# Gated cross-attention and a routed feed-forward layer: a second buffer of unloaded values, positions behind the maxima, tile rows loaded ahead of weights, tiles from the last values' round on

## The chip, the cores and the metric

The kernel runs on one core of a Trainium2 chip. The time is device microseconds from start to end of one execution; the number of the kernel before is the median of three. The engines are TensorE (PE in the profile, its weight loads PEld), VectorE (DVE), ScalarE (ACT), GpSimd (POOL) and the sync engine (SP), which here issues the plain transfers.

## What is computed

Inputs: x of 32 batches x 128 rows x 128 channels, a context of 32 x 120 x 128, one mask of 128 x 120, 16 heads of 8 channels, 8 experts of width 512. Cut to what matters:

```python
x = x + tanh(g_x) * attention(layernorm(x), ctx, ctx, mask)     # 16 heads, softmax over 120 keys
# feed-forward, top 2 of 8 experts, on all 4096 rows
x_flat = layernorm(x).reshape(T, d)
scores = x_flat @ gate_w + gate_b
topk_vals, topk_idx = top_k(scores, 2)
combine_w = zeros.at[tok, topk_idx].add(softmax(topk_vals))
h = relu(x_flat @ w1[e] + b1[e]);  y = h @ w2[e] + b2[e]        # for each expert e
x = x + tanh(g_f) * sum_e combine_w[:, e] * y[e]
```

The kernel computes only the two chosen experts of each row: the rows are scattered to lists in DRAM, one list for each expert (`zs`), read back in tiles of 256 rows, taken through one expert's weights, scattered to `res`, and added at the end.

## The kernel before, in words

**Attention.** 32 batches in 8 groups of 4. The program is written by hand as 38 rounds k = 0 to 37 on every engine (`round_`); G = k // 4 is the group and p = k % 4 the place in it. Round k < 32 takes the row maxima (VectorE, L1068), the exponentials (ScalarE, L819) and the transposes (TensorE, L632, into the banks T and U, copied out to `PT` by L1074 and L826) of batch k. It also takes the products with the values and the row sums of batch k-1 (L654, L664, bank O) and unloads them (`unload`: reciprocal L1080, product into `OT` L1084). At p = 1 TensorE multiplies the group's `OT` by the output weights (`proj_entry`, L673), and VectorE adds the residual (L1089).

**Routing.** For each group VectorE finds the top 2 (`route` parts 0 and 1), makes one-hots and running counts (part 2), adds the ranks that TensorE computed (`RANK`, part 3), makes the row numbers `posu` (part 4, L1142 to L1147) and the weights of the two experts (part 5, L1151 to L1154). GpSimd scatters the normalised rows with `posu` (L959), eight indirect transfers for a group.

**Tiles.** 39 tiles of 256 rows in two batches of tiles: 16 of the groups 0 to 5, and 23 of the rest. A batch's tables (`table` parts 0, 1 and 2, after the last group's ranks) say for each tile its expert and its first row. SP reads them and loads the weights of a tile (`load_w`, 578 KB, 4 buffers) and its rows (`load_z`, 132 KB, 6 buffers); both transfers stand in SP's one queue. TensorE takes a tile in two halves: transposes of the rows (L746), the first product with two banks of hidden values (L718), ScalarE's relu (L856), the second product (L740); VectorE copies the transposed rows (L1221, L1225) and writes the result (L1231), and GpSimd scatters it (L970). One half of a tile is a pair of steps; `PAIRS = 4` of them are planned into each round after the attention's end, up to round 37, and what is left follows. The first rows of a batch of tiles are transposed by opening steps (`PRE`) at the end of the round before the first planned pair.

**Banks.** Steps that are planned before round 33 (`LATE`) use bank O for the rows and results and bank U for the hidden values alone. From round 33 on, O and S0, and U and T, are used in turns.

**The end.** When all tiles are scattered, the results are read back in 16 parts and combined with the weights, and x is stored.

## Time and profile before

| | |
|---|---|
| median of 3 runs | 508.17 us (506.07 to 510.29) |
| the profiled execution's own time | 506.01 us |
| its span, first to last instruction | 504.2 us |
| TensorE busy | 418.4 us (83%) |
| VectorE, ScalarE, GpSimd busy | 268.6, 284.4, 271.8 us |
| mean granted TensorE clock | 0.931 of full speed |

The profile lists for each engine what it ran and when, and for an idle stretch what ended it ("issue" and "remote" are ends for which it shows no releasing instruction). Matmuls are pipelined, so durations of neighbours overlap by some tenths of a microsecond, and the distance between starts is the better measure of pace. Work of the attention rounds ends at about 300 us, tiles run from there to 478 us, and the combination of the results takes the rest.

### The profile page before, as it was taken

The page shows a single profiled execution, that of the slowest core. Times are in us where ns is not written, and L with a number is a line of the kernel's source. Part 1 is how long each engine was busy: PE and PEld are TensorE (multiplying, and loading weights), DVE is VectorE, ACT ScalarE, POOL GpSimd, SP SyncE. Part 2 cuts the span into 40 slices and gives each one's busy share as a digit, 9 for nine tenths or more (in the row PEclk, how much of TensorE's full clock was granted, in tenths as well). Part 3 has the DMA queues.
Part 4 walks back from the last instruction along what each step waited for, and adds up shares of the span by engine and source line. Part 5 has one row for each costly group of instructions (what it writes and reads, how often), then busy time and mean ns, then how long its engine had stood idle before and what let it go on. Part 6 is the DMA issues. An engine that isn't in the chain of part 4 may idle for free.

```text
span 504.2 us, 12347 instructions
## 1 busy us (share of the span) xinstructions
PE 418.4 (83%) x4299; PEld 333.3 (66%) x4299; DVE 268.6 (53%) x1010; ACT 284.4 (56%) x848; POOL 271.8 (54%) x297
## 2 busy tenths in 40 slices
PE   0779889999899999998988777988589999999900
PEld 0455667667667667576756466977479899999800
DVE  1345667777677676776667553433422333233247
ACT  1277868778787778786856711423133444444334
POOL 8536319059498496793942801864755355554500
PEclk9979999999999999999989956998879999999965
DMA  3999999500000000000010052555538677778278
GB/s 74 240 359 410 412 392 216 104 12 14 23 12 23 25 12 23 13 13 29 8 33 14 33 179 81 175 167 168 173 117 251 197 218 233 239 217 247 90 231 280
DMA packets 48155, 72.55 MB, mean 144 GB/s; under 512 B 8054, under 2 KB 32638, under 8 KB 48094
## 3 DMA queue, kind: packets, MB, share of 16 engines
q1 hardware_dynamic: 43549, 62.32, 40.6%
q0 software_dynamic: 4544, 9.45, 5.3%
q8 instruction: 35, 0.57, 0.5%
q14 instruction: 27, 0.21, 0.1%
HBM read 41.83 MB, written 34.66 MB: 152 GB/s over the span
## 4 chain that ended last, share of the span: by engine, by line
PE 74%; issue 8%; DVE 5%; DMA 4%; ACT 3%; SPq 3%; POOL 1%; another core or an unknown queue 1%; DVEq 0%; POOLq 0%; ACTq 0%
PE S L740 7%; PE T L718 7%; PE O L740 7%; PE U L718 7%; PE S L624 6%; PE O L664 6%; PE O L654 6%; PE T L632 6%; PE S L614 5%; PE U L632 5%; ACT P L819 2%; DMA yg<-res 2%; DVE PT L1074 2%; PE E L673 2%; PE E L688 2%
## 5 line engine op out<-in xcount | busy, mean ns | idle before, releaser
L819 ACT ACTIVATE P<-S,nmax 128x120 f32<-128x120 f32 x512 | 135.2, 420 | 6.9 <-DVE nmax L1068 5.4
L959 POOL DMA_INDIRECT zs<-z,posu x64 | 63.2, 988 | 99.6 <-DVE posu L1147 81.0
L970 POOL DMA_INDIRECT res<-yo,dpos x78 | 75.0, 961 | 64.7 <-DVE yo L1231 56.6
L1068 DVE TENSOR_REDUCE nmax<-S 128x4 f32<-128x480 f32 x128 | 75.1, 649 | 37.4 <-PE S L624 32.3
L826 ACT COPY PT<-U 120x512 f32<-120x512 f32 x64 | 39.6, 619 | 52.9 <-PE U L632 51.7
L856 ACT ACTIVATE H<-T,wbuf 128x256 f32<-128x256 f32 x78 | 32.7, 471 | 62.5 <-PE T L718 45.0
L614 PE MATMUL S<-mb_r,I_r 128*128 128x480 f32 x128 | 65.3, 514 | 2.1 <-ACT P L819 1.9
L856 ACT ACTIVATE H<-U,wbuf 128x256 f32<-128x256 f32 x78 | 32.7, 471 | 51.7 <-PE U L718 37.3
L938 POOL TENSOR_SCALAR Kb<-Kt,hm 128x480 f32<-128x480 f32 x32 | 47.0, 1482 | 18.2 <-ACT Kt L840 18.2
L928 POOL TENSOR_SCALAR z<-X,mv,rstd 128x128 f32<-128x128 f32 x64 | 50.2, 791 | 3.0 <-POOL rstd L923 2.7
L1080 DVE RECIPROCAL orec<-O 128x128 f32<-128x128 f32 x32 | 30.6, 957 | 39.2 <-PE O L664 39.2
L718 PE MATMUL T<-zT,wbuf 128*128 128x256 f32 x156 | 42.5, 397 | 6.8 <-issue 6.8
L740 PEld LDWEIGHTS S<-wbuf,H 128*128 128x128 f32 x312 | 42.1, 198 | 8.3 <-issue 6.2
L740 PE MATMUL S<-wbuf,H 128*128 128x128 f32 x312 | 43.4, 284 | 4.6 <-issue 2.9
L664 PE MATMUL O<-PT,oneV 120*32 120x128 f32 x1024 | 41.8, 279 | 5.6 <-issue 5.4
L632 PEld LDWEIGHTS U<-I,P 128*120 128x120 f32 x256 | 30.3, 142 | 24.2 <-issue 22.5
L632 PE MATMUL T<-I,P 128*120 128x128 f32 x256 | 40.9, 284 | 5.3 <-DVE PT L1074 4.1
L654 PE MATMUL O<-PT,Vm 120*32 120x128 f32 x1024 | 35.6, 279 | 11.0 <-issue 11.0
L740 PEld LDWEIGHTS O<-wbuf,H 128*128 128x128 f32 x312 | 41.0, 193 | 4.0 <-DVE yo L1231 2.0
L740 PE MATMUL O<-wbuf,H 128*128 128x128 f32 x312 | 41.6, 276 | 1.4 <-DVE yo L1231 1.4
L632 PE MATMUL U<-I,P 128*120 128x128 f32 x256 | 41.9, 288 | 0.0
L718 PE MATMUL U<-zT,wbuf 128*128 128x256 f32 x156 | 41.8, 392 | 0.0
(161 smaller groups left out, 654.0 us busy)
## 6 DMA issues: line engine op xcount, KB each, us to landing
wbuf<-wpk SPq DMA_DIRECT2D x39, 578.0 KB
zs<-zero SPq DMA_DIRECT2D x1, 17952.0 KB, 60.2
zin<-zs SPq DMA_DIRECT2D x39, 132.0 KB
yg<-res SPq DMA_DIRECT2D x16, 256.0 KB, 4.2
wpk<-in_w SPq DMA_DIRECT2D x1, 2048.0 KB, 57.7
wpk<-in_w SPq DMA_DIRECT2D x8, 256.0 KB, 9.3
out<-X SPq DMA_DIRECT2D x16, 128.0 KB, 3.4
ctx_sb<-in_ctx SPq DMA_DIRECT2D x1, 1440.0 KB, 16.8
```

The lines of the kernel that those rows point to most:

```text
L614: mm(Sb[n % NHG][:, 0:HG * LK].rearrange("p (j k) -> p j k", j=HG), I_r[:], mb_r[:].unsqueeze(1).broadcast_to((128, HG, LK)), start=True, ...
L632: last = nc.tensor.transpose(t_bank(n)[0:LK, j * LQ:(j + 1) * LQ], P[:, n % 4, j, :], I[:])
L654: mm(Ob[32 * j:32 * j + 32, 0:LQ], Vm[:, G % 2, i * HG + j, 32 * g:32 * g + 32], PT[:, (NHG * k + g) % NPT, j * LQ:(j + 1) * LQ], start=(g ...
L664: last = mm(Ob[32 * j:32 * j + 32, LQ:2 * LQ], oneV[:, g, :], PT[:, (NHG * k + g) % NPT, j * LQ:(j + 1) * LQ], start=(g == 0), stop=(g == ...
L718: last = mm(u_bank(a)[:, c * TS:(c + 1) * TS], wbuf[:, n % NW, h * 128:(h + 1) * 128], zT[:, n % 2, :], start=True, stop=True)
L740: last = mm(y[:, 2 * 128:3 * 128], H[:, n % 2, c, h * 128:(h + 1) * 128], wbuf[:, n % NW, FF + c * D:FF + (c + 1) * D], start=(c == 0), st ...
L819: ins = nc.scalar.activation(P[:, n % 4, j, :], a[:, j * LK:(j + 1) * LK], ACT.Exp, bias=nmax[:, n % 4, j:j + 1])
L856: nc.scalar.activation(H[:, n % 2, h, :], u_bank(a)[:, c * TS:(c + 1) * TS], ACT.Relu, bias=wbuf[:, n % NW, W_B1 + h:W_B1 + h + 1]).then_i ...
L928: ins = nc.gpsimd.tensor_scalar(dst[:, i, :], batch_x(G, i), mv[:, i, 0:1], r[:, 1, i:i + 1], ALU.subtract, ALU.mult)
L959: nc.gpsimd.indirect_dma_start(out=zs, out_offset=bass.IndirectOffsetOnAxis(ap=posu[:, F, k, i:i + 1], axis=0), in_=z2[:, F % 2, i, :], in ...
L970: nc.gpsimd.indirect_dma_start(out=res, out_offset=bass.IndirectOffsetOnAxis(ap=dpos[:, n % NDP, h:h + 1], axis=0), in_=yo[:, n % NYO, h, ...
L1068: v.tensor_reduce(nmax[:, n % 4, :], Sb[n % NHG][:, 0:HG * LK].rearrange("p (j k) -> p j k", j=HG), AX_X, ALU.max, negate=True).then_inc(m ...
```

## The change

- `OT` has two buffers, and the first unload of group G waits for the output product of group G-2, not G-1.
- On VectorE the row numbers (route part 4, at p = 1) and the expert weights (part 5, at p = 2) stand right behind the row maxima, ahead of the unload.
- The first batch's table part 2 is written in the same round as part 1 (round 30), not one round later.
- SP loads rows and weights of tiles in turns, rows first. The wait for the tables moves to the first rows' load, which also waits for the scatters of group 5.
- The first planned pair of steps is in round 32, the round of the last values, and the opening steps are at the end of round 31. So 24 of the 34 pairs of the first batch of tiles are planned into rounds, where there were 20; the number of pairs is the same.

```diff
--- before.py
+++ after.py
@@ -94,7 +94,7 @@
 
     subs, pre, k = {}, {}, 0
     for b in range(NB):
-        j, k = 0, max(k, GB * (LAST[b] + 1) + 5)
+        j, k = 0, max(k, GB * (LAST[b] + 1) + 4)
         if k < NR:
             pre[k - 1] = b
         while j < SUBS[b] and k < NR:
@@ -304,7 +304,7 @@
         P = sb("P", [128, 4, HG, LK])
         PT = sb("PT", [LK, NPT, HG * LQ])
         orec = sb("orec", [128, LQ])
-        OT = sb("OT", [128, TOK])
+        OT = sb("OT", [128, 2, TOK])
         xb = sb("xb", [128, GB, D])
 
         z2T = sb("z2T", [128, TOK])
@@ -511,8 +511,6 @@
             def load_w(n):
 
                 b, i = tile_of(n)
-                if i == 0:
-                    sp.wait_ge(table_step, NTAB * (b + 1))
                 wait(sp, yo_done, TH * (n - NW + 1))
                 e = sp.value_load(tab[0:1, b, 1, i:i + 1], min_val=0, max_val=NE - 1)
                 sp.dma_start(wbuf[:, n % NW, :], wpk[bass.ds(e, 1)].squeeze(0)).then_inc(w_in[n % NW], 16)
@@ -521,6 +519,7 @@
 
                 b, i = tile_of(n)
                 if i == 0:
+                    sp.wait_ge(table_step, NTAB * (b + 1))
                     for q in range(2):
                         sp.wait_ge(scat[q], 16 * 2 * GB * ((LAST[b] + 1 - q) // 2))
                 if n >= NZ:
@@ -550,12 +549,13 @@
                     known = N0[b + 1]
                     if b + 1 < NB and ROUND_OF.get((b, 2 * TH * (i + 1) - 1), NEVER) > GB * (LAST[b + 1] + 1) + 1:
                         known = N0[b + 2]
-                    while w_next < min(N0[b] + i + NW, known):
-                        load_w(w_next)
-                        w_next += 1
-                    while z_next < min(N0[b] + i + NZ, known):
-                        load_z(z_next)
-                        z_next += 1
+                    while z_next < min(N0[b] + i + NZ, known) or w_next < min(N0[b] + i + NW, known):
+                        if z_next < min(N0[b] + i + NZ, known):
+                            load_z(z_next)
+                            z_next += 1
+                        if w_next < min(N0[b] + i + NW, known):
+                            load_w(w_next)
+                            w_next += 1
             stored(sp, N0[NB])
             for u in range(NU):
                 load_results(u)
@@ -670,7 +670,7 @@
                 a = entry("PROJ", G)
                 pe.wait_ge(o_free, at(G, GB, GB) + 1)
                 for i in range(GB):
-                    last = mm(a[:, i * D:(i + 1) * D], OT[:, i * LQ:(i + 1) * LQ], wo_sb[:], start=True, stop=True)
+                    last = mm(a[:, i * D:(i + 1) * D], OT[:, G % 2, i * LQ:(i + 1) * LQ], wo_sb[:], start=True, stop=True)
                 last.then_inc(e_ready, 1)
 
             def z2_entry(F):
@@ -1079,9 +1079,9 @@
                 G, i = divmod(k, GB)
                 v.reciprocal(orec[:], Ob[:, LQ:2 * LQ]).then_inc(orec_done, 1)
                 dve.wait_ge(orec_done, k + 1)
-                if i == 0 and G >= 1:
-                    ready(dve, "PROJ", G - 1)
-                v.tensor_tensor(OT[:, i * LQ:(i + 1) * LQ], Ob[:, 0:LQ], orec[:], ALU.mult).then_inc(o_free, 1)
+                if i == 0 and G >= 2:
+                    ready(dve, "PROJ", G - 2)
+                v.tensor_tensor(OT[:, G % 2, i * LQ:(i + 1) * LQ], Ob[:, 0:LQ], orec[:], ALU.mult).then_inc(o_free, 1)
 
             def residual(G):
                 ready(dve, "PROJ", G)
@@ -1258,6 +1258,8 @@
                         row_max(NHG * k + g)
                 if p < 2 and first:
                     taken[first[0]](first[1])
+                if 0 < p < 3 and 0 <= G - 2 < NG:
+                    route(G - 2, 4 if p == 1 else 5)
                 if 0 <= k - 1 < B:
                     unload(k - 1)
                 step(ks[1:2])
@@ -1265,8 +1267,8 @@
                     copy_pt(NHG * k)
                 if middle:
                     taken[middle[0]](middle[1])
-                if p < 3 and 0 <= G - 2 < NG:
-                    route(G - 2, {0: 2, 1: 4, 2: 5}[p])
+                if p == 0 and 0 <= G - 2 < NG:
+                    route(G - 2, 2)
                 if p == 1 and G - 2 == NG - 1:
                     route(G - 2, 5)
                 step(ks[3:4])
@@ -1280,7 +1282,6 @@
                 step(ks[7:8])
                 if p == 2 and G - 1 in LAST and G < NG:
                     table(sb_of(G - 2), 1)
-                if p == 3 and G - 1 in LAST and G < NG:
                     table(sb_of(G - 2), 2)
                 if k in PRE:
                     for i, _ in OPENING:
```

TensorE's queue from the end of round 31 on. A line with - is the order before; `zin` rows are the tile rows' transposes, U and T with `I,P` the last transposes of the attention, O the values and sums.

```order
 L632 MATMUL T<-I,P 120x128 x4
-L632 MATMUL U<-I,P 120x128 x4
-L654 MATMUL O<-PT,Vm 32x128 x16
-L664 MATMUL O<-PT,oneV 32x128 x16
 L746 MATMUL O<-I,zin 128x128 x3
-L695 MATMUL E<-Mh,tri 128x32
-L696 MATMUL E<-CU,ones 128x32
-L718 MATMUL T<-zT,wbuf 128x256 x2
-L746 MATMUL S<-I,zin 128x128
-L673 MATMUL E<-wo_sb,OT 128x128 x4
-L718 MATMUL U<-zT,wbuf 128x256 x2
```

```order
+L632 MATMUL T<-I,P 120x128 x4
+L654 MATMUL O<-PT,Vm 32x128 x16
+L664 MATMUL O<-PT,oneV 32x128 x16
+L718 MATMUL U<-zT,wbuf 128x256 x2
+L746 MATMUL O<-I,zin 128x128
+L718 MATMUL U<-zT,wbuf 128x256 x2
+L746 MATMUL O<-I,zin 128x128
+L718 MATMUL U<-zT,wbuf 128x256 x2
+L740 MATMUL O<-wbuf,H 128x128 x4
```

The three opening transposes now stand ahead of the last attention transposes and values. Four halves of tiles, all with bank U, follow the sums directly, and the ranks and the output product of the last groups come after them.

SP's queue from the first load of a tile on, before:

```order
L517 TENSOR_LOAD tab [waits table_step,wpk_done]
L517 ISA x2
L518 ISA
L518 DMA wbuf<-wpk 128x1156
L517 TENSOR_LOAD tab
```

And with the change:

```order
L528 TENSOR_LOAD tab [waits scat0,scat1,table_step,wpk_done]
L528 ISA x2
L529 ISA
L529 DMA zin<-zs 128x2x132
L515 TENSOR_LOAD tab
L515 ISA x2
L516 ISA
L516 DMA wbuf<-wpk 128x1156
```

Before, four weight loads and then six row loads follow each other. Now the first load is one of rows, behind the table and behind the scatters (`scat0`, `scat1`), and weights and rows alternate.

VectorE's queue in round 29 (p = 1 of group 7), before:

```order
L1080 RECIPROCAL orec<-O 128x128
L1084 TENSOR_TENSOR OT<-O,orec 128x128
L1074 COPY PT<-T 120x512
L1089 TENSOR_TENSOR X<-E,xb 128x512
L1142 TENSOR_TENSOR pm<-hot,pe 128x64
L1143 TENSOR_REDUCE posf<-pm 128x8
L1145 COPY z<-tokf 128x4
L1146 COPY z<-idxf 128x4
L1147 CAST posu<-posf 128x8
```

And with the change:

```order
L1142 TENSOR_TENSOR pm<-hot,pe 128x64
L1143 TENSOR_REDUCE posf<-pm 128x8
L1145 COPY z<-tokf 128x4
L1146 COPY z<-idxf 128x4
L1147 CAST posu<-posf 128x8
L1080 RECIPROCAL orec<-O 128x128
L1084 TENSOR_TENSOR OT<-O,orec 128x128
L1074 COPY PT<-T 120x512
L1089 TENSOR_TENSOR X<-E,xb 128x512
```

The five instructions of `posu` moved from behind the residual to ahead of the reciprocal; the same happens in each p = 1 round from group 2 on.

## Rows read from the trace of the kernel before

**Rows 1.** The page, part 1: busy time, share of the span, instructions.
```profile
PE 418.4 (83%) x4299; PEld 333.3 (66%) x4299; DVE 268.6 (53%) x1010; ACT 284.4 (56%) x848; POOL 271.8 (54%) x297
```
**Rows 2.** The chain that ended last, 440 to 504 us: start, length, what.
```profile
461.69 0.86 PE T L718 x4
...
465.42 0.86 PE T L718 x4
...
479.42 2.23 DMA res<-yo,dpos
...
483.10 5.30 DMA yg<-res
```
**Rows 3.** TensorE in time, around the attention's end: start, length, instruction, [idle before].
```profile
294.31 1.08 PE L632 MATMUL U<-I,P 128*120 128x128 f32 x4
...
297.79 1.96 PE L664 MATMUL O<-PT,oneV 120*32 120x128 f32 x32
305.05 0.66 PE L746 MATMUL O<-I,zin 128*128 128x128 f32 x2 [5.30 <-DMA zin<-zs]
306.62 0.47 PE L746 MATMUL O<-I,zin 128*128 128x128 f32 x1 [0.91 <-DVE zT L1221]
...
307.18 2.05 PE L718 MATMUL T<-zT,wbuf 128*128 128x256 f32 x4
...
309.24 1.91 PE L673 MATMUL E<-wo_sb,OT 128*128 128x128 f32 x8
...
312.25 1.03 PE L718 MATMUL T<-zT,wbuf 128*128 128x256 f32 x4
```
**Rows 4.** SP's queue in time, the first loads of tiles.
```profile
294.64 3.73 SPq L518 DMA_DIRECT2D wbuf<-wpk  x4
299.20 6.59 SPq L530 DMA_DIRECT2D zin<-zs  x6
```
**Rows 5.** Busy time in stretches; last three columns: granted clock, DMA share, GB/s.
```profile
288.00:312.00 24.00, 16.59 (x118) 13.32 (x118) 9.13 (x47) 2.70 (x6) 1.69 (x2) 0.51 0.42 137
290.00:296.00 6.00, 5.39 (x26) 4.69 (x24) 4.42 (x28) 1.75 (x4) 0.00 (x0) 0.50 0.10 17
...
300.00:305.00 5.00, 0.00 (x0) 0.00 (x0) 2.31 (x9) 0.00 (x0) 0.00 (x0) 0.50 0.91 309
...
360.00:374.00 14.00, 7.81 (x32) 6.36 (x32) 1.65 (x10) 2.52 (x6) 8.30 (x10) 0.63 0.35 95
```
**Rows 6.** Who waited for whom over the span: us in total, times, longest.
```profile
DVE OT L1084 <- PE E L673: 6.0, 7, 0.9
...
PE T L632 <- DVE PT L1074: 4.1, 13, 0.4
```
**Rows 7.** VectorE in time, one p = 1 round of the attention.
```profile
199.61 0.96 DVE L1080 RECIPROCAL orec<-O 128x128 f32<-128x128 f32 x1 [1.42 <-PE O L664]
201.43 0.29 DVE L1084 TENSOR_TENSOR OT<-O,orec 128x128 f32<-128x128 f32 x1 [0.86 <-PE E L673]
```
**Rows 8.** TensorE in time, the same round.
```profile
202.46 0.62 PE L632 MATMUL T<-I,P 128*120 128x128 f32 x4 [0.27 <-DVE PT L1074]
```
**Rows 9.** VectorE in time, rounds 29, 31 and a round of tiles.
```profile
272.87 0.16 DVE L1147 CAST posu<-posf 128x8 uint32<-128x8 f32 x1
...
293.38 0.16 DVE L1195 TENSOR_TENSOR st<-end,nt 128x8 f32<-128x8 f32 x1
...
333.14 0.22 DVE L1214 SCALAR_TENSOR_TENSOR dsum<-zin,exf 128x2 f32<-128x2 f32 x1 [4.81 <-remote]
```
**Rows 10.** GpSimd in time: the last scatter of group 5.
```profile
287.46 0.96 POOL L959 DMA_INDIRECT zs<-z,posu  x1 [0.30 <-issue]
```
**Rows 11.** ScalarE in time: the second half's relu.
```profile
312.34 0.84 ACT L856 ACTIVATE H<-U,wbuf 128x256 f32<-128x256 f32 x2 [2.23 <-PE U L718]
```
**Rows 12.** VectorE in time, behind round 37.
```profile
364.95 0.16 DVE L1218 TENSOR_TENSOR dpos<-dsum,own 128x2 uint32<-128x2 f32 x1 [6.89 <-remote]
```
**Rows 13.** GpSimd in time: the last scatter of group 7.
```profile
361.75 0.96 POOL L959 DMA_INDIRECT zs<-z,posu  x1 [0.30 <-issue]
```

## The prediction, made before the changed kernel ran

> **What bounds the kernel now.** I began with the page. TensorE is busy 83% of the span [rows 1], so it is the engine to follow, and I read the chain that ended last. In its last third it is TensorE alone, and from the first half of one tile to the first half of the next it takes 465.42 - 461.69 = 3.73 us [rows 2]. At that pace 39 tiles are 145.5 us. The first product of a tile starts at 307.18 us [rows 3], and the read-back that follows the last tile's scatter starts at 483.10 us [rows 2]. The tiles' stretch is therefore some 30 us longer than its pace, and only such excess, or an idle place before 307 us, can be won. Nothing in the change touches the pace, and nothing touches the 21 us behind 483 us.
>
> Next I went through TensorE in time around the attention's end. The last transposes start at 294.31, the last sums end at 299.76, and then the engine stands still for 5.30 us until the first tile rows land, and for another 0.91 us on VectorE's copy of them [rows 3]. SP's queue says why: the tables are finished at 293.54 [rows 9], four weight loads of 578 KB are issued from 294.64, and the first rows only from 299.20 [rows 4]. While TensorE stands, the DMA engines are 91% busy at 309 GB/s [rows 5]: the rows wait behind 2.3 MB of weights. Last I read the granted clock: from 288 to 312 us it is 0.51, that is the lower of the two levels, 1.2 GHz, and TensorE is busy 16.59 us in it [rows 5]. About half of that, 8.3 us, is what the slow clock costs.
>
> **The change, part by part.**
>
> *Second buffer of `OT`.* In seven p = 1 rounds VectorE waits for the output product before it may write `OT`, 6.0 us in all [rows 6]. In the round shown the wait is 0.86 us [rows 7], and behind it stands the copy of `PT`, for which TensorE then waits 0.27 us [rows 8]. VectorE itself has slack elsewhere. So I count TensorE's wait: 7 x 0.27 = 1.9 us, which with the waits at p = 0 (these stay) makes up the 4.1 us of 13 waits [rows 6]. Bounds: 0, if TensorE waits a little later for ScalarE instead, and 6.0, if all of VectorE's wait reached the end. I take **-1.9**, since TensorE's own row is nearest.
>
> *Positions and expert weights behind the maxima.* Part 4 takes some 0.7 us and stands now where VectorE waits 1.42 us for the sums anyway [rows 7]: 0. In round 29 `posu` comes earlier. Before, it started at 272.87 [rows 9]; it can be some 4 us sooner, and with the shorter wait for `OT` the whole of GpSimd's work behind it moves by about 1.7 us. The last scatter of group 5, issued at 287.46 to 288.42 [rows 10], would then end at 286.7.
>
> *Tables in round 30.* The eight instructions of part 2 (about 1.4 us) move from round 31, where VectorE had long been waiting, to ahead of round 31's maxima. VectorE is about 1.5 us earlier there by the two changes above. They cancel: 0, with bounds of -0.3 and +1.4. The tables are finished near 282 instead of 293.5, and no longer set the start. What is late next is the last scatter.
>
> *Rows first, and the opening in round 31.* A scatter lands about 2.5 us behind GpSimd's instruction (the last one of the program: 479.42 + 2.23 [rows 2], after its end at 479.1). So SP is released near 289.2, issues the first rows near 290.3 (1.1 us from release to issue, as from 293.54 to 294.64 [rows 4, 9]), then weights, rows, weights, one each us. The first rows land near 293, before TensorE comes to them at about 294.3 minus the attention's gain. The second rows stand behind one load of 578 KB, 1.9 us at 309 GB/s, and land near 295.6. So the opening holds TensorE, with the last transposes queued behind it, for about **1.6 us**: from 294.3 to 295.9. Sums end near 301.4, where they ended at 299.76. From there tiles follow without the standstill, since the first weights landed near 295.3.
>
> In round 32 there is one bank for hidden values and one for results. The second half's product waits for the relu of the first, and the third's for that of the second: 0.84 us [rows 11] and a hand-over, about 0.95 us each. In the fourth a second product fills the wait. With products of 2.05 us at the low clock [rows 3], the first starts at 301.4, the second at 304.5, the third at 307.5. Before, the third started at 312.25 [rows 3]. The output product and the ranks, by then done before (1.91 us at the low clock [rows 3], some 1.3 us for both at full clock), are still to come. That is 4.75 - 1.3 = 3.5 us ahead. It shrinks to 1.6 us if the clock stays low until 311 as before, for then 3.8 us of the work after 307.5 runs at half pace. It grows to 4.8 if the clock is back by 303.5, when the third product starts near 306.2. Before, the clock came back some 6 us after TensorE resumed at 305.05; now it has nearly dense work from 297.7 on, so I take a return near 304 and **-4.0**.
>
> *Later.* Four pairs more are done before round 37, so the second batch's tables and scatters come about two tiles later in the sequence of tiles. They still lie ahead of its first tile: cost 0, with one risk below. The other stalls among the tiles I leave as they are, which is a choice: they are neither removed nor added by any edit.
>
> Sum: -1.9 - 4.0 = **-5.9 us**. The profiled execution took 506.01 us and its span was 504.2, so it would become 500.1 and the span 498.3. The median of the runs shown is 2.16 us above the profiled execution. I carry that over: 508.17 - 5.9 = **502.3 us**, 1.2% less.
>
> **A rule against the trace.** From 290 to 296 us TensorE is busy 5.39 of 6 us and its clock is 0.50 all the while [rows 5]; busy time alone did not bring the clock back. The Trainium skill ("TensorE: Matmul & The Clock Gate", Part 1: The HAM clock gate) has the gate open again after sustained busy time; by that rule the new, gapless round 32 would run at full clock early on. I give that way a chance below, priced from rows.
>
> **The rivals.**
>
> 1. *Clock back at once.* The standstill is what kept the clock low, and with dense work it is full from about 298 on. Then 3.4 us of the last values, sums and first product come off as well: -9.3, or 498.9. For it: the standstill. Against it: 290 to 296. Chance 0.15, with the ways in which one of the present stalls happens to vanish.
>
> 2. *The gain is eaten.* TensorE does not resume earlier in effect: VectorE's wait was slack (0 of the 1.9), or the clock stays low to 311 (1.6 of the 4.0). 508.17 - 1.6 = 506.6, at the middle of this case 505.5. Chance 0.20.
>
> 3. *A stall of the other sort, and slower than before.* Twice among the tiles VectorE starts late though TensorE had delivered, by 4.81 and 6.89 us, and the profile shows no engine that released it [rows 9, 12]. From 360 to 374 us TensorE was busy 7.81 of 14 us at a mean clock of 0.63 [rows 5]: 6.2 us idle and about half of 5.8 lost to the clock, 9.1 us for one stall. I suspect that the engine waits for its program while the transfers are dense. The change puts ten loads under the last attention round, where instructions are many. One stall more gives 502.3 + 9.1 = 511.4; it decides once it costs over 5.9 us. If it comes with case 2, the time is near 515. Chance 0.13. The Trainium skill ("Runtime: NRT & Kernel Launch", Instruction fetch mechanics) has the crossing of a block of instructions mostly hidden; by that rule such a stall would be priced at zero and the forecast would stand.
>
> 4. *Weights behind rows.* SP now comes to the second batch's first rows (tile 16) before the weights of tile 15, and waits there for the scatters of group 7. Before, the last was issued at 361.75 [rows 13], about 12 us after `posu`. With the rounds two tiles further on, these weights would land about when tile 15 starts. If late, by up to one load of 3.7 us: 506. Chance 0.07.
>
> The forecast itself: 0.45.
>
> **How the numbers follow.** The measurement can tell about 1% of this kernel from no change. The forecast's own range is 500 to 505, the edges from the clock's bounds and the 1.9. Going out to the other cases I take **495 to 510**: the low end is the forecast with both upper bounds (-4.1 for `OT` and -3.4 for the clock), the high end goes into case 3 up to a stall slightly smaller than the one measured. Faster by over 1% is below 503.1: some 0.32 of the forecast's 0.45, all of case 1 and little of the rest, 0.49. Slower by over 1% is above 513.3: the worse half of case 3, 0.07. The rest is 0.44.
>
> **What would show it.** In the changed kernel's profile: no wait of `OT` for the output product, and seven waits fewer of TensorE for `PT`; the first tables finished near 280; the first rows' load ahead of the first weights' and issued near 288; a wait of about 1.6 us of TensorE at the opening transposes in round 31; the first product within 2 us of the last sums and two gaps of some 0.9 us after it; full clock near 302; the last tile some 6 us earlier. I would be wrong if the opening waited over 5 us (scatters later than I think), if the clock stayed low past 310, or if a stall of several us without a releaser turned up at a place where there is none now.

## The result, and the profile after

The changed kernel took a median of 512.97 us (511.00 to 515.51, 11 runs), beside 508.17 us (505.27 to 510.29, 11 runs) before: ratio 1.0102, 95% interval 1.0079 to 1.0126. The forecast was 502.3 us, 1.2% less; it is 1% more. The sign was wrong. The profiled execution took 514.38 us with a span of 512.6.

The page, first busy time, then part 2's rows of TensorE, its clock and the DMA engines:

```profile
PE 420.0 (82%) x4299; PEld 334.4 (65%) x4299; DVE 268.3 (52%) x1010; ACT 285.2 (56%) x848; POOL 271.5 (53%) x297
...
PE   0688999998998897997998868998739999999900
...
PEclk9979999999899999999999966999779999999965
DMA  3999999500000000000000054565437677777368
```

The work is the same [rows 1]. What the average hides is a ripple of 8s and 7s in the slices from 115 to 256 us, where no transfer of note runs: those are attention rounds, which the prediction touched only with a credit. A second look is at marks: TensorE's start at the same instruction in both traces. I name the values (L654) by their batch k; they are computed in round k + 1, so those of batch 11, the last of its group, stand in round 12, at p = 0.

| mark | before | after | ahead (-) or behind (+) |
|---|---|---|---|
| values of batch 8 | 98.60 | 97.97 | -0.6 |
| values of batch 28 | 267.01 | 277.46 | +10.5 |
| last but one group of four attention transposes (`T`, L632; below: the late transposes) | 293.34 | 301.89 | +8.6 |
| third product of the tiles (L718) | 312.25 | 315.89 | +3.6 |
| opening of the second batch (L746 x2) | 390.55 | 398.81 | +8.3 |
| end of the span | 504.2 | 512.6 | +8.4 |

So three things happened. Twenty attention rounds cost 11.1 us more, of which 1.9 came back by the late transposes. The tiles' start won 4.9 us (14.00 us from the late transposes to the third product, where it was 18.91). The tiles behind it gave 4.6 us back.

**In the attention.** TensorE in time from the values of batch 11 on, after (start, length, instruction, [idle before]):

```profile
123.27 1.08 PE L654 MATMUL O<-PT,Vm 120*32 120x128 f32 x32
124.16 1.13 PE L664 MATMUL O<-PT,oneV 120*32 120x128 f32 x19
125.61 0.42 PE L664 MATMUL O<-PT,oneV 120*32 120x128 f32 x3 [0.32 <-issue]
126.33 0.44 PE L664 MATMUL O<-PT,oneV 120*32 120x128 f32 x4 [0.29 <-issue]
...
127.81 0.38 PE L664 MATMUL O<-PT,oneV 120*32 120x128 f32 x2 [0.29 <-issue]
...
128.69 1.06 PE L632 MATMUL T<-I,P 128*120 128x128 f32 x4
...
134.92 1.08 PE L654 MATMUL O<-PT,Vm 120*32 120x128 f32 x32 [0.59 <-issue]
```

The same instructions before:

```profile
123.25 1.08 PE L654 MATMUL O<-PT,Vm 120*32 120x128 f32 x32
124.15 1.06 PE L664 MATMUL O<-PT,oneV 120*32 120x128 f32 x32
...
125.46 0.60 PE L632 MATMUL T<-I,P 128*120 128x128 f32 x4
...
130.88 1.08 PE L654 MATMUL O<-PT,Vm 120*32 120x128 f32 x32 [0.59 <-issue]
```

The 32 small matmuls of the sums went out in one run of 1.06 us. Now 19 go out and the rest drip, two to four at a time, with 0.3 us between, "issue": no engine is waited for. Then the next transposes take 1.06 us for four, not 0.60, which is the lower clock. From these values to the next is 11.65 us, where it was 7.63. This happens at the values of batches 11, 15, 19 and 23, in the first rounds (p = 0) of groups 3 to 6. Before, it happened in the twenty rounds once, at batch 27, 255.18 to 267.01. In both traces it happens once more at batch 30, behind the twenty rounds: 12.9 us to the next values before (from 283.24), 14.5 us after (from 292.81, a DMA wait of 1.85 us in it). What stands beside it is GpSimd. The first and the last of its four scatters there, after, then before:

```profile
122.93 1.10 POOL L959 DMA_INDIRECT zs<-z,posu  x1 [0.17 <-issue]
...
126.86 0.96 POOL L959 DMA_INDIRECT zs<-z,posu  x1 [0.30 <-issue]
```

```profile
127.18 1.10 POOL L959 DMA_INDIRECT zs<-z,posu  x1 [0.18 <-issue]
...
131.11 0.96 POOL L959 DMA_INDIRECT zs<-z,posu  x1 [0.30 <-issue]
```

With `posu` earlier the whole stream of GpSimd stands 4.25 us earlier. The burst of four began 3.9 us behind the values; now it begins 0.3 us ahead of them and lies across the sums. The slow places of before fit: at batch 27 the burst began at 254.41 and the values at 255.18, and at batch 30 six scatters of group 5 run from 280.90 to 288.42, across the sums from 284.11 on. That is a coincidence in two traces, and the experiments below were made to test it.

**At the tiles' start** the walk of the prediction is seen nearly as written. SP's queue, then TensorE in time, after:

```profile
299.46 0.44 SPq L529 DMA_DIRECT2D zin<-zs  x1
300.66 0.37 SPq L516 DMA_DIRECT2D wbuf<-wpk  x1
301.80 0.38 SPq L529 DMA_DIRECT2D zin<-zs  x1
```

```profile
301.89 1.06 PE L632 MATMUL T<-I,P 128*120 128x128 f32 x4
...
305.22 0.45 PE L746 MATMUL O<-I,zin 128*128 128x128 f32 x1 [1.85 <-DMA zin<-zs]
...
310.86 1.89 PE L718 MATMUL U<-zT,wbuf 128*128 128x256 f32 x4
...
313.77 1.10 PE L718 MATMUL U<-zT,wbuf 128*128 128x256 f32 x4 [0.91 <-ACT H L856]
...
315.89 2.04 PE L718 MATMUL U<-zT,wbuf 128*128 128x256 f32 x4 [0.91 <-ACT H L856]
...
362.06 2.04 PE L718 MATMUL T<-zT,wbuf 128*128 128x256 f32 x4 [4.09 <-DVE zT L1225]
...
379.99 2.04 PE L718 MATMUL T<-zT,wbuf 128*128 128x256 f32 x4 [7.80 <-DVE zT L1225]
```

One wait of 1.85 us at the opening (forecast 1.6), the first product right behind the sums, two gaps of 0.91 us (forecast 0.95). The 5.30 us of standstill [rows 3] are gone. The last two rows are the price: TensorE waits for VectorE, and VectorE and ScalarE wait for nobody that the profile shows. In the list of waits, among the tiles, before and after (engine, line: us in total, times, longest):

```profile
ACT H L856 <- remote: 10.6, 3, 5.0
DVE dpos L1218 <- remote: 6.9, 1, 6.9
```

```profile
ACT H L856 <- remote: 14.6, 4, 6.3
DVE dpos L1218 <- remote: 13.3, 3, 6.6
```

### The profile page after: what moved, and what is told of

Same layout as the page of the kernel before. It is cut to its first block, busy times and chain, and to the rows that moved or that the text cites. A ratio compares the mean times of both kernels' runs of the same rounds, so it can differ in the third digit from the quotient of the medians.

```text
span 512.6 us, 12346 instructions
## 1 busy us (share of the span) xinstructions
PE 420.0 (82%) x4299; PEld 334.4 (65%) x4299; DVE 268.3 (52%) x1010; ACT 285.2 (56%) x848; POOL 271.5 (53%) x297
## 4 chain that ended last, share of the span: by engine, by line
PE 68%; DVE 8%; issue 6%; another core or an unknown queue 4%; DMA 4%; POOL 3%; ACT 3%; SPq 2%; DVEq 0%; POOLq 0%; ACTq 0%
PE U L718 7%; PE S L740 7%; PE T L718 6%; PE O L740 6%; PE S L624 6%; PE O L664 6%; PE O L654 5%; PE T L632 5%; PE S L614 5%; PE U L632 5%; DMA yg<-res 2%; ACT P L819 2%; DVE orec L1080 2%; DVE nmax L1068 2%
## 5 line engine op out<-in xcount | busy, mean ns | idle before, releaser
L856 ACT ACTIVATE H<-U,wbuf 128x256 f32<-128x256 f32 x82 | 34.4, 471 | 58.4 <-PE U L718 46.1
L856 ACT ACTIVATE H<-T,wbuf 128x256 f32<-128x256 f32 x74 | 31.1, 471 | 53.2 <-PE T L718 31.9
L664 PE MATMUL O<-PT,oneV 120*32 120x128 f32 x1024 | 45.2, 278 | 8.2 <-issue 7.7
L718 PE MATMUL T<-zT,wbuf 128*128 128x256 f32 x148 | 40.5, 398 | 13.3 <-DVE zT L1225 12.4
L632 PE MATMUL T<-I,P 128*120 128x128 f32 x260 | 42.6, 289 | 7.9 <-DVE PT L1074 6.6
L718 PE MATMUL U<-zT,wbuf 128*128 128x256 f32 x164 | 45.0, 399 | 1.8 <-ACT H L856 1.8
L632 PEld LDWEIGHTS U<-I,P 128*120 128x120 f32 x252 | 29.6, 141 | 24.2 <-issue 22.5
L654 PE MATMUL O<-PT,Vm 120*32 120x128 f32 x1024 | 35.8, 279 | 11.6 <-issue 10.9
L740 PEld LDWEIGHTS O<-wbuf,H 128*128 128x128 f32 x320 | 42.6, 195 | 3.4 <-issue 1.1
L740 PE MATMUL O<-wbuf,H 128*128 128x128 f32 x320 | 43.1, 278 | 0.7 <-issue 0.7
L632 PEld LDWEIGHTS T<-I,P 128*120 128x120 f32 x260 | 32.1, 144 | 17.0 <-issue 10.5
L740 PE MATMUL S<-wbuf,H 128*128 128x128 f32 x304 | 42.0, 283 | 1.1 <-ACT H L856 0.9
```

The lines of the kernel that those rows point to most:

```text
L632: last = nc.tensor.transpose(t_bank(n)[0:LK, j * LQ:(j + 1) * LQ], P[:, n % 4, j, :], I[:])
L654: mm(Ob[32 * j:32 * j + 32, 0:LQ], Vm[:, G % 2, i * HG + j, 32 * g:32 * g + 32], PT[:, (NHG * k + g) % NPT, j * LQ:(j + 1) * LQ], start=(g ...
L664: last = mm(Ob[32 * j:32 * j + 32, LQ:2 * LQ], oneV[:, g, :], PT[:, (NHG * k + g) % NPT, j * LQ:(j + 1) * LQ], start=(g == 0), stop=(g == ...
L718: last = mm(u_bank(a)[:, c * TS:(c + 1) * TS], wbuf[:, n % NW, h * 128:(h + 1) * 128], zT[:, n % 2, :], start=True, stop=True)
L740: last = mm(y[:, 2 * 128:3 * 128], H[:, n % 2, c, h * 128:(h + 1) * 128], wbuf[:, n % NW, FF + c * D:FF + (c + 1) * D], start=(c == 0), st ...
L856: nc.scalar.activation(H[:, n % 2, h, :], u_bank(a)[:, c * TS:(c + 1) * TS], ACT.Relu, bias=wbuf[:, n % NW, W_B1 + h:W_B1 + h + 1]).then_i ...
```

## The experiments

The theory after the first look was: **(T)** scatters that fall on TensorE's run of values and sums slow the arrival of its instructions; the earlier `posu` put them there. Rivals: the bytes of the scatters or their alignment do it; the second `OT` buffer does it; the tiles' part does it.

One thing must be known to read the numbers. The kernel before had medians of 508 to 511 us in three sessions and the first measurement, and of 476 us in two sessions, 1 and 4 below. In those two the drip of matmuls at the sums is absent from every trace. What makes the difference is not known; the number of the chip does not tell it, since sessions 1 and 5 both have chip 4. I compare only within a session. "Before" is its median there.

### Session 1 (before 476.57 us)

*The changed kernel with the positions (part 4) at their old place.*

```
-                if 0 < p < 3 and 0 <= G - 2 < NG:
-                    route(G - 2, 4 if p == 1 else 5)
+                if p == 2 and 0 <= G - 2 < NG:
+                    route(G - 2, 5)
...
-                if p == 0 and 0 <= G - 2 < NG:
-                    route(G - 2, 2)
+                if p < 2 and 0 <= G - 2 < NG:
+                    route(G - 2, {0: 2, 1: 4}[p])
```

> The changed kernel with the row numbers (route part 4) back behind the residual, as before; all else of the change stays. Theory (the early row numbers let GpSimd run some 4 us ahead, and its four scatters in a row then fall on TensorE's values and sums): the stretch between the values of batch 4G-1 and of batch 4G is 7.6 us again in every group (11.6 us in groups 3 to 6 of the changed kernel), and the time is near the kernel before, 504 to 509. Rival (TensorE waits longer for copies because VectorE's order or the second buffer of OT is worse): nothing comes back, 511 to 515. Rival (the loss is in the tiles' start): nothing comes back either.

480.08 us, ratio 1.008 (1.0048 to 1.0112).

*The kernel before with the positions at the new place, nothing else.*

```
+                if p == 1 and 0 <= G - 2 < NG:
+                    route(G - 2, 4)
                 if 0 <= k - 1 < B:
                     unload(k - 1)
...
-                if p < 3 and 0 <= G - 2 < NG:
-                    route(G - 2, {0: 2, 1: 4, 2: 5}[p])
+                if p in (0, 2) and 0 <= G - 2 < NG:
+                    route(G - 2, {0: 2, 2: 5}[p])
```

> The kernel before with one edit, the row numbers (route part 4) ahead of the unload at p = 1. Theory: the four scatters fall on values and sums in some or most groups, 4 us for each, so 508 + 4 to 16 = 512 to 522, with TensorE's gaps of 0.3 us in the sums at the time of the scatters. Rivals (VectorE's other changes, or the tiles' start): 507 to 510, no such gaps.

475.19 us, ratio 0.9977 (0.9962 to 0.9991).

*The changed kernel, the bursts at p = 0 held until the last round's sums are through TensorE.*

```
                 F, parts = SCATTERS[p]
+                if p == 0 and 0 <= G + F < NG and G + F + 1 not in LAST:
+                    pool.wait_ge(pv_done, min(k, B))
```

> The changed kernel, and GpSimd waits at p = 0 for the sums of the batch before it issues the four scatters. The row numbers stay early. Theory (collision in time): the stalls in groups 3 to 6 go, 504 to 508, though the early row numbers stay. Rival (VectorE's order costs the time): the scatters' place does not matter, 511 to 515.

476.15 us, ratio 0.9991 (0.9966 to 1.0015).

*The changed kernel, rows of 576 bytes instead of 528 (each starts on 64 bytes).*

```
-ZW, Z_TOK, Z_EXP = D + 4, D, D + 1
+ZW, Z_TOK, Z_EXP = D + 16, D, D + 1
```

> The changed kernel with rows of 144 instead of 132 numbers (576 bytes, so that each row in DRAM starts at a multiple of 64 bytes). The number of scatters and their moments stay. If the stalls come from rows of 528 bytes that straddle such pieces in DRAM, the gaps in the sums and the starts without a releaser among the tiles shrink or go: 490 to 505. If they come from the scatters' number and their descriptors, or from GpSimd's work, the time stays at 511 to 515 (a little more, for 9% more bytes).

476.33 us, ratio 1.0000 (0.9974 to 1.0025).

What follows: nothing on the theory, since the disturbance was not there. From the values of batch 8 to those of batch 28 the three with two `OT` buffers need 158.3 us and the one with a single buffer 161.1, and no sums drip. Bursts lie on the sums here too (in the second kernel the one at batch 11 begins 1.1 us behind the values) and cost nothing. The early positions cost nothing then. That bounds them: alone they are a small gain (-0.23%), and their price in the first measurement comes wholly with the drip. The 0.8% of the first kernel I could not place in full: it reaches the tiles' opening 0.9 us later than the third kernel (281.81 against 280.94), and waits 1.27 us for `z` at 318.97.

Three of the four show what rival 4 named. TensorE in time in the third kernel:

```profile
353.92 1.79 PE L718 MATMUL T<-zT,wbuf 128*128 128x256 f32 x4 [3.49 <-DMA wbuf<-wpk]
```

The weights of tile 15 come late, behind the rows of tile 16 and the scatters that those wait for. In the first and the fourth kernel the wait is 3.64 and 3.09 us.

### Session 2 (before 510.75 us)

*The changed kernel, unaltered.*

> The changed kernel itself, once more, since the runs of this study do not all come from the chip of the first comparison: in the last runs the kernel before took 476.6 us, not 508.2, and no engine started late without a releaser. Theory (the loss is such stalls, called up where scatters fall on dense stretches of instructions): where the stalls are there, about 1% slower than before; where they are not, no slower, 470 to 477. Rival (the order itself is worse): 1% slower on either.

521.36 us, ratio 1.0162 (1.0087 to 1.0238).

*The held p = 0 bursts again* (the edit is that of the third kernel above).

> The changed kernel with GpSimd's four scatters at p = 0 held back until the sums. Theory: where there are stalls, 4 to 16 us less than the changed kernel; where there are none, the same as the changed kernel within 1 us. Rival (another cause than the collision): no difference on either.

513.9 us, ratio 1.0052 (1.0025 to 1.0079).

*The 576-byte rows again.*

> The changed kernel with rows of 576 bytes. If the stalls come from rows that straddle pieces of 64 bytes in DRAM, they shrink where they are there. Else, and where there are none, no difference from the changed kernel beyond 1 us.

519.75 us, ratio 1.0144 (1.0075 to 1.0213).

*The kernel before with the tiles' part alone*: SP's order, the tables in round 30, and the opening one round earlier, as the diff of the change has them, without its hunks on `OT` and `route`.

```
-        j, k = 0, max(k, GB * (LAST[b] + 1) + 5)
+        j, k = 0, max(k, GB * (LAST[b] + 1) + 4)
...
                     table(sb_of(G - 2), 1)
-                if p == 3 and G - 1 in LAST and G < NG:
                     table(sb_of(G - 2), 2)
```

> The kernel before with the tiles' part of the change alone (rows first in SP's queue, tables in round 30, opening in round 31, pairs from round 32), without the second buffer and with the old places of the row numbers. Forecast's walk: 4 us less than before. What the last traces show: the opening waits some 7 us for scatters and rows with the last values queued behind it, so the gain is 0 to 2 us. Rival (this part is the loss): 3 us or more slower than before.

510.6 us, ratio 0.9986 (0.9961 to 1.0010).

What follows: the loss is back and so is the drip. Holding the larger of the two bursts of a group takes off 1.1 points of it; alignment takes off nothing that these intervals tell apart. The tiles' part alone is worth nothing, and costs nothing either: from the late transposes to the third product it needs 14.15 us, as the change does, and from the late transposes to the second batch's opening 100.15 us, where before needed 97.21. Its list of waits among the tiles:

```profile
ACT H L856 <- remote: 21.0, 4, 7.2
DVE dpos L1218 <- remote: 15.7, 3, 9.4
```

### Session 3 (before 511.44 us)

*The changed kernel with the positions at their old place again.*

> The changed kernel with the row numbers back behind the residual, once more, for a chip on which the stalls occur. Theory (GpSimd's scatters fall on the sums): the four scatters start 3.7 us behind the start of the values of batch 4G-1 again instead of 0.3 us ahead of it, no stall in groups 3 to 6, 10 to 16 us less than the changed kernel (521.4 on the chip of the last comparison), so 505 to 511. Rival: stays near the changed kernel. On a chip without stalls: 480 again.

503.62 us, ratio 0.9844 (0.9797 to 0.9891).

*The kernel before with the positions at the new place again.*

> The kernel before with the row numbers ahead of the unload alone. On the chip without stalls its four scatters started 1.1 us behind the start of those values, and it was 0.2% faster. Theory: where stalls occur, 1 to 4 us in each of four groups, so 4 to 16 us slower than before (515 to 527). Rival (VectorE's order is harmless and so is GpSimd's moment): 508 to 511.

527.6 us, ratio 1.0301 (1.0217 to 1.0384).

*The kernel before with the second `OT` buffer alone.*

```
-        OT = sb("OT", [128, TOK])
+        OT = sb("OT", [128, 2, TOK])
...
-                if i == 0 and G >= 1:
-                    ready(dve, "PROJ", G - 1)
+                if i == 0 and G >= 2:
+                    ready(dve, "PROJ", G - 2)
```

> The kernel before with the second buffer of OT alone. Forecast: 1.9 us less, with 6.0 as the upper bound. GpSimd's scatters move by 0.9 us at most, so no more stalls: 3.5 us less (the groups' periods on the chip without stalls were 31.7 us with the buffer and 32.3 without). Rival (the earlier start of the next round's work shifts the scatters into the sums): 0 or slower.

504.32 us, ratio 0.9878 (0.9828 to 0.9928).

*The changed kernel, the scatters at p = 0, 1 and 3 held until the last sums are through TensorE.* The last group of each batch of tiles (groups 5 and 7) scatters from another place of the program, without the wait.

```
                     for part in parts:
+                        if part == parts[0]:
+                            pool.wait_ge(pv_done, min(k, B))
                         scatter(G + F, part, GB)
```

> The changed kernel, and GpSimd waits for the sums of the round before the scatters at p = 0, 1 and 3, not at p = 0 alone. Theory: the stall that remained behind the held-back scatters (8.8 us from values to values where 7.6 is the rule, and 9.2 where 8.4 is) shrinks further, so 3 to 6 us less than with p = 0 alone, 508 to 511. Rival (what remained is not from the scatters): 513 to 516.

499.94 us, ratio 0.9769 (0.9705 to 0.9833).

What follows: these four bear the theory out. The positions' edit alone makes the kernel before 3% slower; taken out of the change, it turns +1.0 or +1.6% (first measurement and session 2) into -1.6%. The `OT` buffer alone gives -1.2%; 3.5 us had been expected, and the medians are 7.1 apart. With the tiles' 0 of session 2 the parts add up to +1.7%, beside the whole's +1.6% there. And the edit may stay if only the scatters are kept off the sums: then the change is 2.3% faster. 508 to 511 us had been expected; it is 499.94. GpSimd waits, and up to 260 us TensorE's waits for "issue" at the sums go. Batch 11 in that kernel, TensorE and then GpSimd in time:

```profile
121.17 1.08 PE L654 MATMUL O<-PT,Vm 120*32 120x128 f32 x32
122.06 1.06 PE L664 MATMUL O<-PT,oneV 120*32 120x128 f32 x32
...
123.38 0.60 PE L632 MATMUL T<-I,P 128*120 128x128 f32 x4
...
129.18 1.08 PE L654 MATMUL O<-PT,Vm 120*32 120x128 f32 x32 [0.97 <-issue]
```

```profile
124.24 1.10 POOL L959 DMA_INDIRECT zs<-z,posu  x1 [0.17 <-issue]
125.64 0.96 POOL L959 DMA_INDIRECT zs<-z,posu  x1 [0.30 <-issue]
```

At batch 30, where the wait does not stand, group 5's six scatters run from 272.53 to 279.99 us and the sums drip still:

```profile
276.69 0.47 PE L664 MATMUL O<-PT,oneV 120*32 120x128 f32 x7
278.22 0.43 PE L664 MATMUL O<-PT,oneV 120*32 120x128 f32 x4 [1.06 <-issue]
```

And batch 11 in the kernel before with the positions' edit alone (burst from 123.34 us):

```profile
123.76 1.08 PE L654 MATMUL O<-PT,Vm 120*32 120x128 f32 x32
124.66 1.11 PE L664 MATMUL O<-PT,oneV 120*32 120x128 f32 x16
126.10 0.39 PE L664 MATMUL O<-PT,oneV 120*32 120x128 f32 x3 [0.34 <-issue]
126.83 0.43 PE L664 MATMUL O<-PT,oneV 120*32 120x128 f32 x5 [0.34 <-issue]
```

The same over the sessions with a drip: start of the burst less start of the values at batch 11, TensorE's idle time ahead of the sums put down to issue (us, 40 to 260 us of the span) and how often, the 20 rounds from the values of batch 8 to those of batch 28, and the ratio to before in its own session.

| kernel | burst - values | issue at sums, times | 20 rounds | ratio |
|---|---|---|---|---|
| before | +3.9 | 2.1, 7 | 168.4 | 1 |
| the change | -0.3 | 5.1, 17 | 179.5 | 1.010 |
| the change, session 2 | -0.4 | 9.8, 26 | 187.8 | 1.016 |
| before, positions new | -0.4 | 10.3, 27 | 192.2 | 1.030 |
| the change, positions old | +3.7 | 3.1, 5 | 164.1 | 0.984 |
| the change, p = 0 bursts held | +2.3 | 2.7, 9 | 176.1 | 1.005 |
| the change, scatters at p = 0, 1, 3 held | +3.1 | none listed | 161.1 | 0.977 |
| before, two `OT` buffers | +3.7 | 2.9, 6 | 164.1 | 0.988 |
| before, the tiles' part | +3.9 | 3.9, 7 | 168.7 | 0.999 |

With the p = 0 bursts held, the pair of scatters at p = 3 stays: it begins at 114.46, the values of batch 10 at 114.36, and the next values come 8.93 us later, not 7.6.

The idle time named issue is only part of a stall: 1.2 us at batch 11 after, and 4.0 us lost. Most of the loss is there already when the transposes behind the sums start (128.69 for 125.46, 3.2 us). It is not the clock: TensorE's granted clock is 1.00 from 125 to 128 us. The lower clock comes behind it (0.50 from 129 to 131 us, 1.06 for 0.60 us of transposes), and with VectorE and ScalarE late in turn it has what is left, 0.8 us.

### Session 4 (before 476.3 us)

*The scatters held as in session 3's last kernel, and SP loads weights ahead of rows from the fifth tile's weights on.*

```
+                        if n_w(i) and w_next < min(N0[b] + i + NW, known):
+                            load_w(w_next)
+                            w_next += 1
                         if z_next < min(N0[b] + i + NZ, known):
                             load_z(z_next)
                             z_next += 1
-                        if w_next < min(N0[b] + i + NW, known):
+                        if not n_w(i) and w_next < min(N0[b] + i + NW, known):
```

(`n_w(i)` is `w_next >= NW`.)

> The changed kernel with all scatters of attention rounds behind the sums, and with SP taking the weights before the rows again from the fifth tile's weights on. Theory: the wait of 3.5 us for the weights of tile 15, which stood behind the rows of tile 16 on the chip without stalls, goes; where stalls in the tiles are longer than that wait it gains nothing. So 0 to 3.5 us less than with the scatters' waits alone (2.3% under before): 2.3 to 3.0% under before. Rival (that wait only takes the place of another): no difference.

472.05 us, ratio 0.9910 (0.9893 to 0.9926).

*The scatters held alike, SP's order as in the change.*

> The changed kernel with the scatters behind the sums, once more beside the others. 2.3% under before where stalls occur; on a chip without them about 0.1% under before, as with the waits at p = 0 alone.

476.08 us, ratio 0.9993 (0.9976 to 1.0009).

*The kernel before with the second `OT` buffer and the scatters held alike.* The edits are the two shown in session 3, and nothing of the tiles' part.

> The kernel before with the second buffer of OT and the scatters behind the sums: neither early row numbers nor the tiles' part. If the tiles' part and the early row numbers are worth nothing beside these, it equals the changed kernel with the same waits (2.3% under before); if the tiles' part gains the forecast's 4 us, it lies 0.8% behind it.

471.76 us, ratio 0.9911 (0.9882 to 0.9941).

*The changed kernel, scatters an eighth as long.* It scatters 16 of the 132 numbers of a row, to a list of its own, so the tiles work on rows of zeros; the results' memory is filled once at the start.

```
-                            out=zs, out_offset=bass.IndirectOffsetOnAxis(ap=posu[:, F, k, i:i + 1], axis=0),
-                            in_=z2[:, F % 2, i, :], in_offset=None).then_inc(scat[F % 2], 16)
+                            out=zq, out_offset=bass.IndirectOffsetOnAxis(ap=posu[:, F, k, i:i + 1], axis=0),
+                            in_=z2[:, F % 2, i, 0:16], in_offset=None).then_inc(scat[F % 2], 16)
```

> The changed kernel; the scatters of the normalised rows carry 16 of 132 numbers and go to a list of their own, so the tiles work on rows of zeros (and the results' memory is filled once at the start). The scatters' number, moments and rows are as before, their bytes an eighth. If the stalls come from the bytes written, those in the sums go: about 3% under the changed kernel. If they come from the number of descriptors or from GpSimd's writing of them, they stay, and so does the time.

477.16 us, ratio 1.0016 (0.9997 to 1.0035).

What follows: without the drip the short rows say nothing. The others settle the tiles' part where there is no drip. Without the mend of SP's order the change's whole gain is lost to the wait for tile 15's weights, 3.71 us at 355.74 us. With the mend two shorter waits are left, the last two of these rows (the first is the third product):

```profile
293.55 1.10 PE L725 MATMUL U<-zT,wbuf 128*128 128x256 f32 x4 [0.91 <-ACT H L863]
...
357.01 1.13 PE L725 MATMUL T<-zT,wbuf 128*128 128x256 f32 x4 [0.50 <-DMA wbuf<-wpk]
...
360.94 1.13 PE L725 MATMUL T<-zT,wbuf 128*128 128x256 f32 x4 [1.72 <-DMA wbuf<-wpk]
```

The kernel without the tiles' part has its third product at 295.71, and from 300 to 460 us no wait of TensorE above 0.5 us. So the tiles' part is 2.16 us ahead at the third product, and 2.22 us of waits for weights take it back. The two kernels are equal (0.9910 and 0.9911). The pair was not run in a session with the drip, so what the mended tiles' part is worth there is open.

### Session 5 (before 510.36 us)

*The best kernel again, and the short rows again.*

> The changed kernel with the scatters behind the sums and the weights of tile 15 ahead of the rows of tile 16, for a chip with stalls. There the same kernel without the second edit was 2.3% under the kernel before, and in its trace no wait for weights showed, so theory: 2 to 3% under before again. On a chip without stalls: 0.9% under before again.

497.65 us, ratio 0.9753 (0.9710 to 0.9796).

> The changed kernel with scatters of 16 of 132 numbers, into a list of their own (the tiles work on rows of zeros), for a chip with stalls; there the changed kernel was 1.0 to 1.6% slower than before. If the stalls hang on the bytes: 1 to 3% under before, no gaps in the sums. If on the number of descriptors: 1 to 1.6% over before, with the gaps.

522.36 us, ratio 1.0226 (1.0150 to 1.0302), from two runs.

What follows: the scatters of an eighth of the bytes disturb TensorE as much as the full ones (9.5 us of issue at the sums, 26 times; 184.8 us for the 20 rounds). So the bytes are not the cause. A burst of four costs more than a pair (mostly 8.4 to 9.2 us to the next values beside the pair at p = 3, 11.3 to 13.8 beside four), but GpSimd works longer on it too, and no run tells these apart. The version that beats both kernels is the change with the scatters held and SP's order mended: -2.5% here (2 to 3% expected), and -0.9% in session 4.

## Why the prediction was wrong

**The step that failed** is the one on the positions: "Part 4 takes some 0.7 us and stands now where VectorE waits 1.42 us for the sums anyway [rows 7]: 0", and behind it "the whole of GpSimd's work behind it moves by about 1.7 us". The first half is right. The second saw a move, for the last scatter of group 5, where it was 1.0 us against the values of batch 30 (4.22 us behind them before, 3.21 after). It missed that in the groups before it GpSimd's stream moves too, by 4.25 us at batch 11, priced the move by one effect, an earlier end of the last scatter, and did not ask what the scatters would then lie beside. That term was 0 and is +3.0% alone (session 3), some 16 us. In the first measurement it shows as the 11.1 us of the twenty rounds. The clue was in the trace: from the values of batch 27 to the next it took 11.8 us where the same stretch of the groups before took 7.6, with a burst on the sums, and from those of batch 30 12.9 us, where the kernels of session 1 and 4 without the tiles' part need 6.4. I had read the excess only behind 290 us.

**"neither removed nor added by any edit"**, said of the stalls without a releaser, was the same mistake in general form. Rival 3 had the right kind, "I suspect that the engine waits for its program", and the right sign, but put it under the last attention round with the row loads. It sat in groups 3 to 6, in smaller pieces of some 4 us. At 512.97 us the result is near that rival's 511.4, but not by its mechanism. That the moment of GpSimd's scatters does it is shown by two kernels whose only edit is a wait on GpSimd, and by the one that moves `posu` alone; the wait also moves what GpSimd does behind the scatters, and that they and not this do it is argued from where the gaps lie. Why they do it is open. Rival 3's reason was that the engine waits for its program. If that means blocks of instructions that come late over the instruction queues (0.5% and 0.1% of the DMA engines' time, before as after), the trace speaks against it. At batch 30 after, the drip lasts from 293.68 to 298.00, and from 290 to 299 us the list of DMA queues has one line, that of the scatters:

```profile
q0 software_dynamic: 192, 0.41, 13.3%
```

Before, an instruction packet moved between 122 and 128 us, beside the values and sums of batch 11, and nothing dripped. The Trainium skill ("Runtime: NRT & Kernel Launch", Instruction fetch mechanics) has the crossing of a block mostly hidden. These two places agree with it.

**`OT`'s second buffer.** The mechanism held: no wait for the output product is left. The size was off. -1.9 us was forecast with a bound of -6.0; alone it gave -1.2%, some 6 us (7.1 between the medians), at or beyond that bound. In session 1, without the drip, the 20 rounds need 158.3 us with two buffers and 161.1 with one, 0.56 us a group, twice the 0.27 that TensorE's own row showed. So the wait had reached TensorE along more than the one path. Where the sums drip something comes on top: in that kernel's trace the 20 rounds took 164.1 us, where before took 168.4. The slow stretch at batch 27 is still there (10.7 us for 11.8).

**Tables earlier:** nothing waited for them, as forecast. The instruction that ended at 293.54 before [rows 9] is at 291.21 us; less the 8.6 us by which the attention ran late that is 282.6, where "near 282" was forecast.

**The tiles' start.** The numbers came out to the third product, where 4.9 us were won against 4.0 forecast (with the opening's wait included), but in part by luck. I had TensorE reach the opening at 294.3, from a trace in which the sums of batch 30 had dripped, and took that for its pace. In the changed kernel they dripped again, so the rows were nearly there (1.85 us of waiting for 1.6). In sessions 1 and 4 nothing dripped, TensorE came on time, and the opening waited 6.6 to 7.7 us in all six kernels with the tiles' part, past the 5 us that the prediction gave as a sign of being wrong. In session 1's third kernel:

```profile
280.94 0.66 PE L746 MATMUL O<-I,zin 128*128 128x128 f32 x2 [4.28 <-DMA zin<-zs]
284.19 0.45 PE L746 MATMUL O<-I,zin 128*128 128x128 f32 x1 [2.60 <-DMA zin<-zs]
```

In session 4 the third product is 2.2 us ahead, not 4. The first rows were issued at 299.46, not 290.3, since the attention ran 8.6 us late. The term failed behind the third product as well: a head start lasts only as long as nothing later is tied to something else. Where the sums drip, waits without a releaser took it (4.6 us from the third product to the second batch's opening after, 7.7 in the tiles' part alone); in session 4, weights did. Why they grew with the earlier start I could not settle: no experiment touched the stalls among the tiles.

**Rival 4** was real. Priced at up to 3.7 us, it measured 3.09 to 3.71 in sessions 1 and 4. In the first measurement its place was taken by the other stalls.

**The clock** (rival 1, and the bounds of the tiles' term). Stretches of the change around the start of the tiles: busy time of PE, PEld, DVE, ACT and POOL, granted clock, DMA share, GB/s:

```profile
311.00:313.00 2.00, 1.86 (x5) 1.17 (x5) 1.35 (x4) 0.21 (x1) 0.00 (x0) 0.64 0.81 249
313.00:315.00 2.00, 1.21 (x5) 0.82 (x5) 1.32 (x9) 0.72 (x3) 0.00 (x0) 1.00 0.24 69
315.00:317.00 2.00, 1.11 (x3) 0.96 (x4) 0.42 (x2) 0.75 (x2) 0.00 (x0) 0.71 0.00 0
317.00:319.00 2.00, 2.00 (x9) 1.82 (x8) 0.00 (x0) 0.84 (x2) 0.00 (x0) 0.50 0.00 0
319.00:321.00 2.00, 2.00 (x15) 1.76 (x14) 0.56 (x3) 0.47 (x2) 0.50 (x1) 0.94 0.00 0
```

TensorE resumed at 307.29 and worked densely, and the clock came back some 5 us later. I had allowed some 6 us (dense from 297.7, back near 304), which was the right size. But it fell again behind the two gaps of 0.91 us and came back at 319. So the third product took 2.04 us, and rival 1, full clock at once, is wrong. The Trainium skill ("TensorE: Matmul & The Clock Gate", Part 1: The HAM clock gate) opens the gate after sustained work; the return at 312 agrees. The fall came between 315 and 317 us, behind a stretch from 313 to 315 with TensorE busy 1.21 of 2 us.

## What to carry to other kernels

An edit that costs its own engine nothing still moves every stream that waits for its result: follow that stream to its DMA issues and ask what each will stand beside afterwards. A stall without a releaser that occurs once or twice in the trace of before is a warning, not an oddity: find what else happened beside it, because a move of a few us can make it happen in every group. A time taken from a trace with such a stall in front of it is not the engine's pace. A wait added on an idle engine, to keep its burst of indirect transfers off the densest stretch of small instructions, can be worth more than the work taken off the path.

## What the runs showed that I had not expected

- In the sessions with the drip, a burst of four indirect scatters (0.96 us each on GpSimd, 1.3 us apart) beside TensorE's 64 small matmuls cost some 4 to 6 us a time and a pair mostly 0.8 to 1.6 us, with next to no transfer running (6% of the DMA engines from 110 to 137 us). An eighth of the bytes makes no difference, nor does the rows' alignment.
- The same kernel took 476 us in two sessions and 508 to 511 us in the others (medians). What the traces show of the difference is these drips and the stalls among the tiles. The edit that costs 3% in one session gains 0.2% in another, so a result from a single session could have had either sign.
- After a stall the clock falls to its lower level for a few us (0.50 from 129 to 131 us): the four transposes behind it took 1.06 us instead of 0.60. That adds at most 0.8 us to the 3.2 already lost.
